# Expert stage of a fused token, attention and mixture-of-experts kernel: two tiles of rows per step with gate and up weights stationary

## The reference

```python
xf = rms_norm(x, norm_w).reshape(-1, D)                  # D = 192
probs = softmax(xf @ router_w.T)                         # 8 experts
comb_w = probs * one_hot(top_k(probs, 2)).sum(axis=1)
g = einsum('td,efd->tef', xf, gate_w)                    # D_EXPERT = 384
u = einsum('td,efd->tef', xf, up_w)
h = silu(g) * u * comb_w[:, :, None]
y = einsum('tef,edf->td', h, down_w)
```

## Time and profile before

| | |
|---|---|
| median of 3 runs | 540.03 us (538.32 to 542.23) |
| profiled execution, its own time | 540.32 us |
| its span, first to last instruction | 538.6 us |
| PE busy | 480.9 us, 89% |
| DVE busy | 375.9 us, 70% |
| ACT busy | 304.9 us, 57% |
| POOL busy | 189.0 us, 35% |
| mean granted TensorE clock | 0.971 of 2.4 GHz |

### The profile page before, as it was taken

How to read it: one execution, slowest core, us unless ns; L and a number is a source line. 1 busy time by engine, 2 the same in 40 slices (tenths; PEclk the granted TensorE clock), 3 DMA queues, 4 the chain that set the end, 5 groups by cost and what they waited for, 6 DMA issues and landing times.

```text
span 538.6 us, 12568 instructions
## 1 busy us (share of the span) xinstructions
PE 480.9 (89%) x3157; PEld 456.8 (85%) x3158; DVE 375.9 (70%) x1295; ACT 304.9 (57%) x773; POOL 189.0 (35%) x272
## 2 busy tenths in 40 slices
PE   1999999999898985999999999999999999999800
PEld 1999998777777775899999999999999999999800
DVE  4969996658998899676665565566556556655596
ACT  5493977847788876345444544444454444445473
POOL 1000000004777776753333433333343333334320
PEclk9999999999999999799999999999999999999965
DMA  8989622311433431742222222222223222225897
GB/s 306 413 349 374 186 106 88 149 45 52 119 119 93 140 97 67 171 111 74 72 83 69 69 78 76 69 76 79 69 69 82 72 69 70 84 69 165 262 353 229
DMA packets 62463, 71.67 MB, mean 133 GB/s; under 512 B 19057, under 2 KB 56626, under 8 KB 61410
## 3 DMA queue, kind: packets, MB, share of 16 engines
q1 hardware_dynamic: 49920, 51.43, 31.5%
q0 software_dynamic: 8208, 16.95, 8.8%
q10 hardware_dynamic: 4306, 2.95, 2.0%
HBM read 49.43 MB, written 21.86 MB: 132 GB/s over the span
## 4 chain that ended last, share of the span: by engine, by line
PE 69%; DVE 17%; DMA 6%; ACT 3%; issue 2%; ACTq 1%; SPq 0%; POOL 0%; DVEq 0%; POOLq 0%
PE bank L849 8%; PE pair L849 6%; PE bank L1095 5%; PE bank L1099 5%; PE bank L1097 5%; PE bank L1096 5%; PE bank L1098 5%; PE bank L1106 5%; PE bank L1115 4%; PE pair L1115 4%; PE pair L1084 3%; ACT yall L760 2%; DMA ydram<-ysb,dnow 2%; DVE hres L1373 2%; PE bank L1117 2%
## 5 line engine op out<-in xcount | busy, mean ns | idle before, releaser
L793 POOL DMA_INDIRECT disp<-xf,posu x82 | 82.1, 1001 | 151.6 <-ACT xf L671 128.4
L1590 DVE TENSOR_TENSOR hh<-sg,bank 128x384 f32<-128x384 f32 x89 | 49.3, 554 | 99.3 <-ACT sg L741 99.3
L823 POOL DMA_INDIRECT ydram<-ysb,dnow x89 | 88.5, 994 | 69.5 <-DMA ydram<-ysb,dnow 36.6
L741 ACT ACTIVATE sg<-bank 128x384 f32<-128x384 f32 x89 | 43.8, 492 | 116.4 <-PE bank L1099 116.4
L1095 PE MATMUL bank<-wa,xh 128*128 x178 | 67.6, 380 | 0.0
L1099 PE MATMUL bank<-wa,xl 128*128 x178 | 60.1, 338 | 0.0
L1097 PE MATMUL bank<-wa,xl 128*128 x178 | 59.9, 336 | 0.0
L1096 PE MATMUL bank<-wa,xh 128*128 x178 | 59.8, 336 | 0.0
L1098 PE MATMUL bank<-wa,xh 128*128 x178 | 59.6, 335 | 0.0
L820 POOL COPY dnow<-dest 128x1 uint32 (+1 forms) x89 | 16.6, 187 | 107.4 <-DVE ysb L1600 97.7
L849 PE MATMUL bank<-wcT,imgT 128*128 128x193 f32 x240 | 42.5, 340 | 11.0 <-DMA imgT<-in_pixels 11.0
(11 more groups left out here) (262 smaller groups left out, 1163.8 us busy)
## 6 DMA issues: line engine op xcount, KB each, us to landing
xs<-disp SPq DMA_DIRECT2D x89, 96.0 KB, 2.0
band<-in_bands SPq DMA_DIRECT2D x4, 1536.0 KB, 12.1
yall<-ydram SPq DMA_DIRECT2D x7, 768.0 KB, 7.6
imgT<-in_pixels SPq DMA_DIRECT2D x4, 768.0 KB, 12.9
imgT<-in_pixels SPq DMA_DIRECT2D x2, 1536.0 KB, 16.0
hres<-in_text SPq DMA_DIRECT2D x1, 3072.0 KB, 26.1
wa<-in_gate_up_w SPq DMA_DIRECT2D x8, 384.0 KB, 5.8
ring<-in_gate_up_w SPq DMA_DIRECT2D x32, 96.0 KB, 2.9
```

The costliest lines, as they stand in the source:

```text
L793: pool.indirect_dma_start(disp, bass.IndirectOffsetOnAxis(ap=posu[xbuf(c)][:, 2 * j + k:2 * j + k + 1], axis=0), xfd[xbuf(c)][:, j, :], No ...
L823: pool.indirect_dma_start(ydram, bass.IndirectOffsetOnAxis(ap=dnow[b][:], axis=0), ysb[r][:], None).then_inc(s_ys[b], 16)
L1590: v.tensor_tensor(hh[o][:], sg[o][:], bank[2 * o + 1][:, 0:DE], ALU.mult).then_inc(s_hh, 1)
```

## The change

Of the 89 slots 68 run as 34 steps of two tiles of the same expert (256 rows, called pairs here); six slots ahead of them and 15 behind stay single (lone). There are 55 items: 0 to 5 lone, 6 to 39 pairs (`PAIR0` = 6, `PAIR1` = 40), 40 to 54 lone. The lone ones at the end hold the odd tile of each expert and what full pairs are left over. In a pair:

- Gate and up are made with the weights stationary and the 256 rows streaming: for each third c of the 384 hidden features 10 matmuls of 256 columns, 30 in all. The result lies hidden features by rows, as down wants it, and `turn_hidden` (three transposes per tile) isn't made. `hth` is copied from `hh` in SBUF instead of from PSUM.
- The stationary operand isn't selected by a register: SP copies the gate and up weights of the step's expert from `wa` to a fixed buffer `wnow` by three DMAs of 128x768 floats per step, one for each third c. Each waits until PE is through with the same third of the step before. There is one `wnow`.
- The rows are loaded into `xs[b]`, two buffers of 256 rows instead of four of 128; lone tiles use halves of them.
- `wa` is laid out by thirds (`wa6`), so the loads and the splitting of the weights run over three pieces of 128.
- ACT, DVE and PE get new step programs; DVE works out a longer table for the lone items behind the pairs.

```diff
+FULL = (TILES * 2 - NE) // 2
+FIRST = 6
+PAIR0, PAIR1 = FIRST, FIRST + FULL - FIRST // 2
+NLONE = SLOTS - 2 * FULL
+ITEMS = PAIR1 + NLONE
...
+        sg = at("sg", [P, 2 * DE], F32, r_gh + 18688)
+        wnow = at("wnow", [P, FC * GU], F32R, r_gh + 9280)
...
+        xs = [sb("xs0", [P, 2, 2 * P + 3]), at("xs1", [P, 2, 2 * P + 3], F32, r_xT0 + 64)]
...
+            def load_pair(s, b):
+
+                free_at = s - 2 if isinstance(s, int) and s == PAIR0 else s - 1
+                sp.wait_ge(s_xst, free_at)
+                sp.wait_ge(s_dest, free_at)
+                row = sp.value_load(tab[0:1, 0, bass.ds(s, 1)], min_val=0, max_val=NE * REGION)
+                rows = disp[bass.ds(row, W2), :].rearrange("(j p) d -> p j d", j=2)
+                sp.dma_start(xs[b][:, :, 0:D], rows[:, :, 0:D]).then_inc(s_xs[b], 16)
+
+                sp.dma_start(xs[b][:, :, D:2 * P + 3], rows[:, :, D1:DROW]).then_inc(s_xs[b], 16)
...
+            def copy_expert(i):
+
+                e = sp.value_load(tab[0:1, 1, bass.ds(i, 1)], min_val=0, max_val=NE - 1)
+                for c in range(FC):
+                    if late_enough(i, PAIR0 + 1):
+                        sp.wait_ge(s_gu, blocks(i) + (c - 2))
+                    sp.dma_start(wnow[:, GU * c:GU * c + GU].bitcast(F32),
+                                 wa[:, bass.ds(e * (FC * GU) + GU * c, GU)].bitcast(F32)).then_inc(s_wnow[c], 16)
...
+            load_pair(PAIR0, 0)
+            copy_expert(PAIR0)
+            load_pair(PAIR0 + 1, 1)
+            copy_expert(PAIR0 + 1)
+            with sp.Fori(0, (PAIR1 - PAIR0 - 2) // 2) as i:
+                for b in range(2):
+                    load_pair(2 * i + (PAIR0 + 2 + b), b)
+                    copy_expert(2 * i + (PAIR0 + 2 + b))
             sp.wait_ge(s_tab, 3)
...
+            for i in range(PAIR1, ITEMS):
+                load_lone(i)
...
+            def gate_up_pair(i, b):
+
+                pe.wait_ge(s_xlo, i + 1)
+                x = [(xh[b][:, W2 * m:W2 * m + W2], xl[b][:, W2 * m:W2 * m + W2]) for m in range(2)]
+                for c in range(FC):
+                    at_front = isinstance(i, int) and i == PAIR0
+                    pe.wait_ge(s_hh, blocks(i) + (min(c - 1, 0) if at_front else c - 2))
+                    pe.wait_ge(s_wnow[c], 16 * i + (16 - 16 * PAIR0))
                     for which in range(2):
...
+                        high, low, rest = (wnow[:, GU * c + W2 * r + P * which:GU * c + W2 * r + P * which + P] for r in range(3))
+                        acc = bank[c][:, W2 * which:W2 * which + W2]
+                        pe.matmul(acc, high, x[0][0], start=True, stop=False)
+                        pe.matmul(acc, high, x[0][1], start=False, stop=False)
+                        pe.matmul(acc, low, x[0][0], start=False, stop=False)
+                        pe.matmul(acc, rest, x[1][0], start=False, stop=False)
+                        ins = pe.matmul(acc, rest, x[1][1], start=False, stop=True)
                     ins.then_inc(s_gu, 1)
...
+            def step(i, b):
+
+                if is_pair(i):
+                    gate_up_pair(i, b)
+                    if is_pair(i + 2) or is_lone(i + 2):
+                        turn_rows(i + 2, b)
...
+                if is_pair(i - 1):
+                    for t in range(2):
+                        down(down_reg[1 - b], 1 - b, tile_of(i - 1) + t, t, P * t, W2, blocks(i - 1) + 3)
```

More of the change, by code:

```diff
@@ L753, in step @@
                     norm_tile(t // CT_TILES, t % CT_TILES)
-            pipeline(act, step, "xsht", (2, 1, 0, -1), peel=4)
+            items(act, step)
             act.wait_ge(s_wts, 1)
@@ new lines, in gate_up_lone @@
+            def gate_up_lone(i, b):
+                e = pe.snap(gate_reg[b], min_val=0, max_val=NE - 1)
+                pe.wait_ge(s_xlo, i + 1)
+                if i > 1:
+                    pe.wait_ge(s_hh, blocks(i) - 1)
+                for which in range(2):
+                    high, low, rest = (wa6[:, bass.ds(e, 1), :, r, which, :].rearrange("p e c f -> p (e c) f") for r in range(3))
+                    acc = lone_banks(i)[which][:, 0:DE].rearrange("p (c f) -> p c f", c=FC)
+                    pe.matmul(acc, xh[b][:, 0:P], high, start=True, stop=False)
+                    pe.matmul(acc, xh[b][:, 0:P], low, start=False, stop=False)
+                    pe.matmul(acc, xl[b][:, 0:P], high, start=False, stop=False)
+                    pe.matmul(acc, xh[b][:, P:2 * P], rest, start=False, stop=False)
+                    ins = pe.matmul(acc, xl[b][:, P:2 * P], rest, start=False, stop=True)
+                ins.then_inc(s_gu, 1)
@@ new lines, in down @@
+            def down(reg, b, g, p, first, step_c, ready_at):
+                e = pe.snap(reg, min_val=0, max_val=NE - 1)
+                pe.wait_ge(s_htl, ready_at)
+                if late_enough(g, 2):
+                    pe.wait_ge(s_y, g - 1)
+                for c in range(FC):
+                    o = first + step_c * c
+                    both = bass.ds(e * (FC * 2 * D) + c * 2 * D, 2 * D)
+                    high = bass.ds(e * (FC * 2 * D) + c * 2 * D, D)
+                    pe.matmul(bank[6 + p][:, 0:2 * D], hth[b][:, o:o + P], wd[:, both], start=(c == 0), stop=False)
+                    ins = pe.matmul(bank[6 + p][:, 0:D], htl[b][:, o:o + P], wd[:, high], start=False, stop=(c == FC - 1))
+                ins.then_inc(s_dn, 1)
@@ L1127, in _ @@
+            items(pe, step)
         @block.vector
@@ L1490, in _ @@
             v.wait_ge(s_cread, 1)
-            cnt, til, cum, gap, one = (ct[:, k, :] for k in range(5))
+            cnt, til, cum, gap, one, full2, odd, cumo = (ct[:, k, :] for k in range(8))
             st.mark(v.memset(one, 1.0))
@@ L1607, in _ @@
+            items(v, step)
             v.wait_ge(s_upd, TILES)
```

446 lines of the change are left out of this document (274 added, 172 removed).

## The result

| | before | after |
|---|---|---|
| median | 539.88 us | 776.59 us (771.6 to 777.9, 4 runs) |
| ratio to before | | 1.436 (95%: 1.428 to 1.445) |
| span of the profiled execution | 538.6 us | 773.9 us |
| PE busy | 480.9 us, 89% | 551.3 us, 71% |
| mean granted TensorE clock | 0.971 | 0.84 |

The kernel is 44% slower. 743 us was predicted, with 660 to 790 as the range; the time is 34 us above the number and inside the range. From the page of after: busy tenths of PE, granted clock and DMA in the 40 slices (of 19.3 us now), the chain that ended last by engine and by line, the costliest group, and the two kinds of DMA of the stage.

What follows compares the result with a forecast made beforehand. TensorE alone was taken to bound the expert stage. 540.3 - 213.5 + 196.5 + 148.5 + 2 = 674 us, plus 69 for the falling clock, gave 743 us; range 660 to 790 us.

Steps and rivals of the forecast that it cites:

- PE's own work, and the table: In the pairs' steps: 5.78 us of PE work against 6.28 for two slots, 17.0 us gained, less 2 for the longer table.
- the wait for the rows: Ahead of the pairs' transposes of rows PE waits 4.5 us a step (4.0 to 6.2), 33 times: 148.5 us.
- the clock: In PE's gaps the clock falls to 0.50, slowing work behind: 2.1 us a step, 69 in all; chance 0.60.
- the price of the load's issue: In SP's queue, from the end of the awaited instruction: 0.91 us to the rows' first DMA, 0.52 more to the second.
- The landing of 2.3 us: The rows' second DMA into xs lands in 1.9 us, plus 0.4 for twice the rows and the copy ahead.
- The rival in which such copies move at half the pace of loads from DRAM: In the DMA engines: slow copies inside SBUF delay the rows behind them, wait 6.2 us, 799 us in all; chance 0.10.
- The copies are hidden: Weight copies into wnow go out some 8 us before use, against 3.5 us for a lone load, so they stay hidden.
- 2.3 us of the low stretch lie in the gap: Of the 6.8 us of low clock a step, 2.3 lie in PE's gap and 4.5 in its work.
- The clock holds: In the pairs' stage the clock stays up and only the 4.5 us wait is paid: 674 us; chance 0.20.
- Faster, the wait is hidden: Ahead of the transposes, rows come so early that PE never waits; 17.0 us gained, 525 us; chance 0.03.

Runs made afterwards that it cites:

- PE kept busy: Changed kernel with 18 matmuls of constants (the fillers) between a pair's gate and up and the transposes of rows; 694.7 us, ratio 1.286.
- load before the last third: Changed kernel with the load of the next pair's rows between the copies of the middle and the last third of the weights; 698.5 us, ratio 1.293.
- load before the middle third: Changed kernel with the load of the next pair's rows between the copies of the first and the middle third; 637.4 us, ratio 1.179.
- kernel before, late loads: Kernel before, but from slot 8 on SP's load of rows waits for gate and up of two slots ahead; 810.3 us, ratio 1.499.
- late loads, PE kept busy: Kernel before with loads of rows delayed from slot 8 on, plus seven matmuls of constants ahead of PE's wait for the rows; 734.3 us, ratio 1.357.

## Why the prediction was right, and by how much it was off

The mechanism held: the rows come late, PE waits for them, and the clock falls in each gap. The runs separate its terms. Going from before by single differences:

| term | predicted | measured | by which runs |
|---|---|---|---|
| PE's own work, and the table | -15 | -19.4 | copies left out, against before |
| the wait for the rows | +148.5 | +174 | PE kept busy (694.7), against copies left out (520.5) |
| the clock | +69 | +82 | the changed kernel (776.6), against PE kept busy |
| sum | 743 | 777 | |

Of the middle line 4 us are the fillers' own, as the step of item 39 shows: the wait is 170 and the clock 86 us. All three terms missed by less than a third of their size, the two large ones both to the low side, so the 34 us aren't a large error hidden by another.

**PE's own work.** 0.12 us was taken for a matmul of 256 columns, on a line between 192 and 384; the timeline has 0.113 to 0.118. A step is 5.68 us instead of 5.78. The 2 us put down for the longer table at the front don't show: 34 x 0.6 us = 20.4 would be gained by the step alone, and 19.4 were.

**The wait, 33 times as counted.** This is the term that was mis-sized most, by some 21 us (170 against 148.5). From the end of PE's last slot of gate and up, 4.5 us were reckoned; it is 4.9 and 5.5 by turns, 5.2 in the mean. The short one agrees well: 2.5 us to the second load's issue (2.2 reckoned) and 2.4 from there to PE (2.3). The long one has another 0.75 us in SP's queue. The step that failed is the price of the load's issue, 0.91 us to the first DMA, read from a load in the kernel before: there SP had been waiting, and nothing was in its queue. Reading the row number alone took 0.28 us there and 0.54 or 0.79 here. Behind a copy it is 1.68 us from the copy's start to the first load's (1.5 reckoned, 0.6 + 0.91), and 2.38 where the loop turns in between. A turn of a loop that holds two steps should have been looked for on the path, once SP's issue was on it.

The landing of 2.3 us, made up of 1.9 for a lone load and 0.4 for twice the rows behind a copy, is right to 0.1 us. The second load of a pair (L517) has:

```profile
DMA to landing us min/median/max: 2.0/2.2/2.5
```

The Trainium skill, DMA: Bandwidth & Descriptors, section Anatomy of one DMA, gives a fit, measured on the path of GpSimd, of 2.0 us plus the bytes at 436 GB/s. By it an estimate for a copy of 384 KB is 2.9 us. The copies here, issued by SP and from SBUF to SBUF, took 2.8 in the middle. The rival in which such copies move at half the pace of loads from DRAM (799 us) is out: with 1.9 us for the landing of a small load, 0.9 is left for the 384 KB, not twice 1.09, and the rows behind them land in 2.2. The instructions on `wnow`:

```profile
DMA to landing us min/median/max: 2.6/2.8/3.6
```

**The copies are hidden** in the changed kernel, as was said: none of PE's gaps lies in front of gate and up. That was true only because the steps had become so long. In steps of 5.7 us they are hidden only just: with SP's queue as the only one, the kernel takes 11 us more than without copies, and without the load in that queue 4.

**The clock.** That it falls in each gap was given 0.60, and is what happened. Its price was put at 2.1 us a step and is 2.6 (86 / 33). The fall was expected 2.2 us into the gap, since the one fall inside the run of before was seen there. Here it comes almost at the gap's end, in each of the 12 steps from 290 to 450 us 0.6 to 1.2 us before it. The step of PE's timeline above by windows, as in the earlier trace rows (the gap goes from 399.9 to 404.7):

```profile
395.00:399.90 4.90, 4.90 (x33) 4.74 (x32) 1.53 (x4) 1.57 (x5) 2.34 (x4) 0.78 0.27 100
399.90:404.00 4.10, 0.05 (x1) 0.00 (x0) 0.76 (x2) 0.52 (x2) 0.00 (x0) 1.00 0.80 279
404.00:404.70 0.70, 0.02 (x1) 0.03 (x1) 0.00 (x0) 0.00 (x0) 0.00 (x0) 0.51 0.06 12
404.70:410.80 6.10, 6.10 (x26) 6.10 (x27) 1.96 (x5) 1.53 (x4) 1.35 (x3) 0.50 0.00 0
410.80:413.00 2.20, 2.20 (x21) 2.20 (x21) 1.02 (x3) 1.07 (x3) 0.98 (x1) 0.99 0.44 165
```

The clock is at 1.00 for 4.1 us of the gap, at half for its last 0.7, and stays there for the next 6.1 us, in which PE works. At the prediction's 0.46 the 6.1 us lose 2.8, and the mean over the 12 steps, with 5.9 us in work, 2.7; the fillers give 2.6. The step that failed is thus that 2.3 us of the low stretch lie in the gap: it is 0.9 in the mean. The stretch of 6.8 us was right, its place was not, and the price lay just above the 2.5 that the prediction gave as its upper case.

The Trainium skill, TensorE: Matmul & The Clock Gate, section HAM oscillation, describes a loop in which each wait for a DMA brings the clock down and every burst starts slow. Here this is what happened, with the low stretch of 6.8 us in each of the steps.

**The rivals.** "The clock holds" (674 us) is out: the granted clock is 0.76 in the stage, and even with it held by fillers the time is 695, because of the longer wait. "Faster, the wait is hidden" (525 us) didn't come about in the changed kernel, for the reason given (the queue's order doesn't allow it), but its price was right: with the order mended the kernel takes 531.5, 526.1 and 524.9 us.

## What to carry to other kernels

When a load is issued by a queue that also holds waiting instructions, ask what stands ahead of it and when that is released: here a DMA that waits for the end of the matmuls, put ahead of the load for the next ones, turned a small gain into a loss of 44%. Moving the load ahead of it gave 1.5% over the kernel before, and 2.6 to 3.0% once that queue had fewer DMAs to issue or its loop fewer turns. Price a gap on TensorE twice, once for its length and once for the slow work behind it; matmuls of constants in the gap tell the two apart on the chip. When issue on a queue gets onto the path, count every instruction of it, the turn of the loop too.

## What was not expected of the hardware

The trace of before showed a fall in a gap of 2.2 us that followed a thinner stretch, and one after 3.4 us. In the runs the clock fell again and again in gaps of that size with nothing but dense work between them. Means over the steps from 290 to 450 us (the gap beyond the usual distance from start to start; the loss is the step less its work, 5.68 or 3.14, and less the gap):

| kernel | gap, us | steps with a low clock | low clock in a step, us | loss in a step, us |
|---|---|---|---|---|
| after | 5.2 | 12 of 12 | 6.8 | 2.8 |
| load before the last third | 3.6 | 14 of 14 | 4.4 | 1.9 |
| load before the middle third | 2.4 | 13 of 18 | 2.5 | 1.2 |
| kernel before, late loads | 2.2 | 18 of 24 | 2.6 | 1.2 |
| late loads, PE kept busy | 0.7 | 0 of 29 | 0 | |
| PE kept busy | 1.0 | 0 of 14 | 0 | |

A gap of 2.2 or 2.4 us in each step was enough to lower the clock in three of four steps, and to cost half its own length once more. In the first row the clock stayed high for some 4 us of idle time and then fell. With the load before the middle third each of the 13 falls came 0.4 to 1.5 us after PE had started again. So the length of the gap alone doesn't say when the clock falls, as the prediction took it to; what does isn't shown. The loss isn't all or nothing: it grows with the gap. Gaps between 1.0 and 2.2 us, and other lengths of work between them, weren't tried. For the changed kernel this table gives 2.8 us of loss a step and the fillers 2.6 over the whole stage. The whole stage agrees with the fillers: from 247.4 to 699.8 us it is 256 us longer than without copies (248.1 to 444.6), and 170 us of that are the 33 gaps, which leaves 2.6 us for each. The steps at its edges lose less than those in the table.

And SP's reading of a number from SBUF took a time that depends on what stands ahead of it. The reads of the kernel before (L479), then in the changed kernel those of the row number behind a copy (L513) and those of the expert behind a load of rows (L538):

```profile
L479 SPq TENSOR_LOAD <-tab x81: 270/276/291, 240.2 to 490.1; - x81
L513 SPq TENSOR_LOAD <-tab x34: 273/564/899, 238.2 to 670.5; - x34
L538 SPq TENSOR_LOAD <-tab x34: 271/280/499, 239.9 to 672.6; - x34
```

Behind a load of rows it takes 0.28 us, as before; behind a copy of 384 KB it took 0.54 in the step shown above, and 0.79 where the loop had turned as well. Why isn't shown.
